# Gate logits taken from extra columns of two products that run anyway, in the second stage of an attention and mixture-of-experts kernel

## The reference

```python
def _mha(x, Wqkv, bqkv, Wo, bo): ...        # 4 heads of 32 
    return o @ Wo.T + bo
def _moe(x, Wg, W1, b1, W2, b2):
    logits = xf @ Wg.T
    idx = jnp.argmax(logits, axis=-1)
    for e in range(E):                       # 8 experts, one per token
        h = jax.nn.relu(xf @ W1[e] + b1[e])
        out = out + m * (h @ W2[e] + b2[e])
y = _layer_norm(x + _mha(x, ...), g1, be1)
z = _layer_norm(y + _moe(y, ...), g2, be2)
```

## Time and profile before

| | us |
|---|---|
| median of 3 runs (lowest, highest) | 1230.01 (1229.64, 1231.98) |
| the profiled execution, its own time | 1225.95 |
| its span in the profile | 1224.1 |
| stage one, until the first transfer of stage two | 803.3 |
| stage two, from there to the last scatter's end | 233.5 |
| of it, slots 6 to 13, mean of one | 12.17 |

### The profile page before, as it was taken

The page is one execution under the profiler, slowest core; times in us unless marked ns, Lnnn a source line. Parts: engine busy times, 40 slices in busy tenths (PEclk is TensorE's granted clock), DMA queues, the critical chain, the costliest instruction groups (busy, mean ns, idle before and its releaser), DMA issues. The chain is left out here.

```text
span 1224.1 us, 49591 instructions
## 1 busy us (share of the span) xinstructions
PE 1099.8 (90%) x17489; PEld 898.3 (73%) x17489; DVE 958.7 (78%) x4172; ACT 922.7 (75%) x3404; POOL 874.6 (71%) x703
## 2 busy tenths in 40 slices
PE   4799999999999999999999999947999972799991
PEld 2688888888888888888888887725877772688881
DVE  6898898998898898898988987546888854376763
ACT  2789989989989889899899897836877641466660
POOL 2777877877877877877777875554677776178885
PEclk9999999999999999999999999969989975799996
DMA  6776766766766666767667666353242124574100
GB/s 197 207 179 158 183 165 167 185 167 161 182 165 172 171 173 166 179 158 181 166 163 183 156 159 180 92 183 93 63 135 92 71 85 161 161 202 138 58 32 25
DMA packets 111027, 180.88 MB, mean 148 GB/s; under 512 B 19726, under 2 KB 64177, under 8 KB 110656
## 3 DMA queue, kind: packets, MB, share of 16 engines
q1 hardware_dynamic: 102944, 158.53, 50.1%
q0 software_dynamic: 6400, 16.82, 3.8%
q10 hardware_dynamic: 1440, 2.36, 0.8%
HBM read 35.20 MB, written 24.73 MB: 49 GB/s over the span
## 5 line engine op out<-in xcount | busy, mean ns | idle before, releaser
L612 POOL TENSOR_TENSOR qk<-mm,sw 128x1024 f32<-128x1024 f32 x128 | 305.1, 2384 | 103.2 <-DMA sw<-mm 102.6
L685 ACT ACTIVATE pr<-sm,mn 128x96 f32<-128x96 f32 x1024 | 368.7, 370 | 0.3 <-DVE mn L513 0.3
L618 POOL TENSOR_TENSOR pr<-pr,ri 128x768 f32<-128x768 f32 x128 | 189.2, 1478 | 66.7 <-DVE ri L540 66.6
L501 DVE TENSOR_TENSOR mm<-bank,cos 128x512 f32<-128x512 f32 x256 | 175.3, 685 | 70.1 <-PE bank L324 58.3
L685 ACT ACTIVATION_READ_ACCUMULATOR pr<-sm,mn 128x1 f32 x1024 | 201.6, 197 | 0.0
L513 DVE CUSTOM_DVE_ANT_0 sm<-bank,msk 128x96 f32<-128x96 f32 x1024 | 190.9, 251 | 3.4 <-PE bank L350 3.4
L502 DVE TENSOR_TENSOR mm<-bank,sin 128x512 f32<-128x512 f32 x256 | 173.8, 679 | 0.0
L377 PE MATMUL bank<-pT,vw 96*64 96x64 f32 x4096 | 148.2, 226 | 0.0
L377 PEld LDWEIGHTS bank<-pT,vw 96*64 96x64 f32 x4096 | 130.6, 138 | 17.2 <-issue 6.0
L676 ACT ACTIVATE pT<-bank 96x512 f32<-96x512 f32 x256 | 137.3, 588 | 0.2 <-PE bank L392 0.2
L392 PE MATMUL bank<-ident,pr 128*96 128x128 f32 x1024 | 133.1, 273 | 0.0
(11 more groups left out here) (206 smaller groups left out, 2485.6 us busy)
## 6 DMA issues: line engine op xcount, KB each, us to landing
sw<-mm SPq DMA_DIRECT2D x512, 128.0 KB, 2.4
vw<-vn SPq DMA_DIRECT2D x128, 192.0 KB, 2.6
vw<-vn SPq DMA_DIRECT2D x128, 128.0 KB, 2.3
rr<-sorted_scratch SPq DMA_DIRECT2D x72, 192.5 KB, 2.6
vw<-vn SPq DMA_DIRECT2D x96, 64.0 KB, 2.2
xt<-in_x SPq DMA_DIRECT2D x16, 256.0 KB, 4.2
x_scratch<-x SPq DMA_DIRECT2D x16, 256.0 KB, 2.6
rr<-x_scratch SPq DMA_DIRECT2D x16, 256.0 KB, 3.2
```

Source lines behind the costliest of these rows:

```text
L501: dve.tensor_tensor(mm[s % 2][:, 0, j, :], PJ[u % 2][:, :], cos[:, :], ALU.mult)
L612: pool.tensor_tensor(qk[i % 2][:, :, 32:], mm[i % 2][:, 0, :, :], sw[i % 2][:, :, :], ALU.add)\
L618: pool.tensor_tensor(t, t, ri[i % 2][:, :].unsqueeze(2).to_broadcast([P, 8, WK]), ALU.mult)\
L685: ins = act.activation(pr[i % 2][:, h, p, :], ms_[i % 2][:, h, p, :], ACT.Exp, scale=-1.0, bias=mn[i % 2][:, h, p:p + 1], accum_out=sums[i ...
```

## The change

Since u is a linear function of the input and of the attention output, the columns of Wg can be carried along. With G = g1 * Wg less its column mean (the norm's mean taken out), the logits are r * (u @ G) + be1 @ Wg. The change

- widens the value product from 128 to 136 columns per group (`wve`: the value weights and G) and the output product likewise (`woe`: the output weights and their product with G); their sum is made by the same addition that makes `uu`, now 4 x 136 wide. Value and output products take two banks each (`wide`), so the ring is laid out anew (`r_pos`, `r_prev`);
- drops the transposes t3, their copy yT, the gate product and the copy of its result; the gate now multiplies eight columns of `uu` by r and adds be1 @ Wg, two DVE operations, and waits for POOL's norm of the same slot;
- moves the gate of a quad from slot s+5 to s+4, rank and scatter from s+6 to s+5: the loops end one slot earlier (20 instead of 21);
- moves the rank counts behind the value product on PE, the be1 x W1 columns into the bank of the output product, `w1l` of an expert to the slot after its high part, and the load of the expert's weights a slot later;
- adds one small ACT copy (eight columns of the value product into `h2`), and lets the input's transposed copy hT be plain, with the biases corrected once (`fbn`) at the stage's start; `prepare()` moves ahead of the first statistics on DVE and a new `gate()` takes its place.

The core of the diff, in the order ring, POOL, PE, ACT, DVE:

```diff
-    FIRST, LAST = -3, NQ + 6
+    FIRST, LAST = -3, NQ + 5
+        for kind, u in (("t1", s), ("q", s), ("k", s), ("pt", s - 2), ("v", s), ("rk", s - 5), ("wo", s - 3)):
+                size = 2 if kind in ("v", "wo") else 1
+                pos += pos % size if kind != "rk" else 1 - pos % 2
...
+                        pool.wait_ge(s_le, 2 * (s - 6) + 1)
...
-                u = s - 6
+                u = s - 5
...
-                u = s - 5
-                    pe.wait_ge(s_cy, u + 1)
-                    dst = bank("t3", u)
-                    for j in range(4):
-                        ins = pe.transpose(dst[:, j * P:(j + 1) * P], quad_rows(u)[:, j, 0:C], ident[:, :])
...
-                    for j in range(4):
-                        ins = pe.matmul(dst[:, j * NE:(j + 1) * NE], yT[:, j * P:(j + 1) * P], wg, start=True, stop=True)
+                    for g in range(4):
+                        ins = pe.matmul(dst[:, g // 2, g % 2, :], hT[u % 2][:, g * P:(g + 1) * P], wve[:, :],
+                                        start=True, stop=True)
...
+                        ins = pe.matmul(dst[:, j // 2, j % 2, :], oT[u % 2][:, j * P:(j + 1) * P], woe[:, :],
                                         start=True, stop=True)
...
-                    act.activation(yT[:, :], ring("t3", u)[:, :], ACT.Identity, scale=gcol[:, 0:1], bias=gcol[:, 1:2])\
-                        .then_inc(s_ye, 1)
+                    act.activation(halves(h2[u % 7][:, :, C:]), blocks("v", u)[:, :, :, C:], ACT.Copy).then_inc(s_ve, 1)
...
+                    dve.tensor_tensor(halves(uu[u % 2][:, :, :]), blocks("wo", u), halves(h2[u % 7][:, :, :]), ALU.add)\
+                        .then_inc(s_u, 1)
...
-                u = s - 5
-                    dve.wait_ge(s_r, r_use[("lg", u)] + 1)
+                u = s - 4
+                    dve.wait_ge(s_ln, norms(s))
...
-                    dve.tensor_copy(lg[:, :, :], ring("lg", u)[:, 0:4 * NE].rearrange("p (j e) -> p j e", j=4))\
+                    dve.tensor_tensor(lg[:, :, :], uu[u % 2][:, :, C:], rs[s % 2][:, 1, :].unsqueeze(2).to_broadcast([P, 4, NE]),
+                                      ALU.mult).then_inc(s_le, 1)
+                    dve.wait_ge(s_le, 2 * u + 1)
+                    dve.tensor_tensor(lg[:, :, :], lg[:, :, :], lgb[:, :].unsqueeze(1).to_broadcast([P, 4, NE]), ALU.add)\
```

More of the change, by code:

```diff
@@ L742, in phase2 @@
     hc = [sbt(p2, f"hc{n}", [P, 4, C]) for n in range(2)]
-    h2 = [sbt(p2, f"h2{n}", [P, 4, C]) for n in range(7)]
+    h2 = [sbt(p2, f"h2{n}", [P, 4, CE]) for n in range(7)]
     hT = [sbt(p2, f"hT{n}", [P, 4 * P]) for n in range(2)]
@@ L754, in phase2 @@
     oT = [sbt(p2, f"foT{n}", [P, 4 * P]) for n in range(2)]
-    uu = [sbt(p2, f"uu{n}", [P, 4, C]) for n in range(2)]
-    yT = sbt(p2, "yT", [P, 4 * P])
+    uu = [sbt(p2, f"uu{n}", [P, 4, CE]) for n in range(2)]
+    wve = sbt(p2, "wve", [P, CE])
+    woe = sbt(p2, "woe", [P, CE])
+    woT = sbt(p2, "woT", [P, C])
+    wgs = sbt(p2, "wgs", [P, NE])
+    lgb = sbt(p2, "lgb", [P, NE])
+    fbn = sbt(p2, "fbn", [P, 3])
     lg = sbt(p2, "lg", [P, 4, NE])
@@ L1018, in bank @@
             def bank(*w):
-                n = r_use[w]
-                if n >= 4:
-                    kind, v = order[n - 4]
+                for kind, v in sorted(r_prev[w]):
                     pe.wait_ge(emptied[kind], v + 1)
-                return RING[n % 4]
+                return ring(*w)
             pe.wait_ge(s_l2, 16 * 6)
@@ L1085, in _ @@
                 if quad(u):
-                    pe.wait_ge(s_cy, u + 1)
-                    dst = bank("t3", u)
-                    for j in range(4):
-                        ins = pe.transpose(dst[:, j * P:(j + 1) * P], quad_rows(u)[:, j, 0:C], ident[:, :])
+                    pe.wait_ge(s_oh, u + 1)
+                    dst = bank("rk", u)
+                    for j in range(5):
+                        o = dst[:, j * NE:(j + 1) * NE]
+                        for i in range(min(j, 3) + 1):
+                            ins = pe.matmul(o, trb[:, 0:P] if i == j else trb[:, P:2 * P], oh[u % 2][:, i, :],
+                                            start=(i == 0), stop=(i == min(j, 3)))
                     ins.then_inc(s_r, 1)
@@ L1120, in _ @@
                     pe.wait_ge(s_oe, 4 * u + 4)
-                    dst = bank("wo", u)
+                    bank("wo", u)
+                    dst = blocks("wo", u)
+                    e = u - 2
+                    if 0 <= e < NE:
+                        pe.wait_ge(s_ws[e % 2], 16 * (e // 2 + 1))
+                        for c in range(4):
+                            pe.matmul(pair("wo", u)[:, 0, 2 * CE + c:2 * CE + c + 1], w1s[e % 2][:, c * P:(c + 1) * P],
+                                      gcol[:, 1:2], start=True, stop=True)
                     for j in range(4):
-                        ins = pe.matmul(dst[:, j * C:(j + 1) * C], oT[u % 2][:, j * P:(j + 1) * P], wfo,
+                        ins = pe.matmul(dst[:, j // 2, j % 2, :], oT[u % 2][:, j * P:(j + 1) * P], woe[:, :],
                                         start=True, stop=True)
@@ L1216, in _ @@
                     act.wait_ge(s_r, r_use[("k", u)] + 1)
-                    act.activation(kT[u % 2][:, :], ring("k", u)[:, :], ACT.Identity, bias=fb[:, 1:2]).then_inc(s_ke, 1)
+                    act.activation(kT[u % 2][:, :], ring("k", u)[:, :], ACT.Identity, bias=fbn[:, 1:2]).then_inc(s_ke, 1)
                 u = s - 2
```

135 lines of the change are left out of this document (71 added, 64 removed).

## The result

The changed kernel took 1236.87 us (median of 20 runs, 1230.74 to 1241.65), the kernel before 1230.99 in runs beside them (20 runs, 1225.23 to 1235.98): a ratio of 1.0049 [1.0034, 1.0064]. The forecast was 1214.6 and faster.

What follows compares the result with a forecast made beforehand. PE was taken to bound slots 6 to 13, DVE close behind, and POOL the end. Gains of 7.2 + 1.1 + 2.0 + 5.1 = 15.4 us gave 1214.6 us, in a range of 1207 to 1224.

Steps and rivals of the forecast that it cites:

- DVE becomes the bound: Slots 6 to 13: PE's cut leaves DVE binding, 12.17 to 11.27 us a slot, 7.2 us gained over eight.
- rival 1: PE stays the bound through its pauses; steady gain 0 to 1 us, whole kernel 1223 us; chance 0.15.
- The clock: Sign of being wrong: PE's granted clock in slots 6 to 13 falls below about 0.85.
- DVE's list: DVE's own work in slots 6 to 13: 10.83 plus 0.24 makes 11.07 us a slot, before 0.2 for rank counts.
- Rival 3: Where POOL is late, its operations hold DVE's gate, about 1 us a slot over ten slots: 1225 us; chance 0.04.
- The other sign: Sign of being wrong: DVE's first gate operation shows idle time behind POOL's norm.
- Rival 2: PE at 1.2 GHz in the whole stage: 19 us lost, 5.1 gained, 1244 us; chance 0.05.
- rival 5: A new bank wait in the ring eats the slots' gain, the norm's wait the end's: 1229 us; chance 0.03.
- The start: Start of stage two: `prepare()` runs in DVE's first wait, POOL's norm covers `gate()`; between -1 and +1, taken as 0.
- The end: From norm(15) to the last scatter's end: POOL's list has one quad of scatters less, 5.1 us gained, between 4 and 8.
- Slots 14 and 15: No expert's weights there, POOL's list binds: 10.6 us a slot, 1.1 us gained, between 0 and 2.
- this term was +2.0: POOL comes out of the steady part less late: 2.0 us gained, between 0 and 3.

Runs made afterwards that it cites:

- 76 records ahead: Changed kernel plus 38 small 32x32 products, results unread, on PE ahead of the slot loop: 1225.49 us, ratio 0.9964 to the kernel before.
- three buffers: Changed kernel with three instead of two buffers for the experts' weights: 1236.22 us, ratio 1.0056 to the kernel before.
- ACT's order: Changed kernel with ACT's copies of keys and transposed probabilities ahead of the exponent: 1233.14 us, ratio 1.001 to the kernel before.
- 300 records ahead: 150 small 32x32 products on PE ahead of the slot loop: changed kernel 1235.95 us (ratio 1.0057), kernel before 1229.43 us (0.9983).
- the last three sets: Runs of both kernels with half the small products, each twice as wide, and of combined edits; the unchanged kernel before took 1278 to 1294 us beside them.
- the first two: Sets with the first four experiments and the scan of records ahead; beside them the kernel before took 1230.56 and 1231.22 us.

## Why the prediction was wrong

*The step that failed* is "DVE becomes the bound", and in it rival 1's answer, "DVE's 2 us of room hide most of a pause". A slot does not end with the longest list of one engine, but with the later of that list and the loop DVE, ACT, PE, DVE. The loop is some 9.7 us long when nothing disturbs it, 1.5 below the list (the estimate above). A pause costs it not 2 us but 4.2, since the products behind it run at the lower clock. Both numbers stood in the earlier trace rows (1.74 of pause, 2.00 for the product); they were never put into the chain that ends at DVE's addition. DVE's waits on PE, 10.7 us in the earlier trace rows, were taken for PE's load, which the cut removes; but the pauses of over 0.8 us in those slots alone sum to 6.3 us (1.68, 0.83, 2.09, 1.74), and their slow rows come on top; these the cut does not remove. This term was +7.2 and measured -7.5. DVE's waits for PE were to be under 0.5 us a slot and were 1.95.

*The clock* was named as the sign of being wrong (below about 0.85) and came to 0.84. The runs add that it falls behind the pause: after three of the four pauses in P by V the next two steps are the slow ones (1.87 and 2.16 us), after the first only the second (1.82). Over 935.80 to 940.00 the granted clock is 0.50. With more work on PE it was 0.87 in slots 6 to 13, and they took as long (104.3 us). The Trainium skill (TensorE: Matmul & The Clock Gate, "A second HAM failure mode: psum-queue depth-cycling") tells of frequent short idle spells that swing the clock; the trace agrees with that much, while in these slots the idle spells in front of the slow rows have no bank or other releaser named.

*Rival 1* was the right mechanism with a chance of 0.15 and too small a price: it let the steady part give back the cut, no more, and came to 1223. That less work makes the records of a slot fewer, and thereby moves where pauses fall, was not in it at all. The place alone is 11 us. Which kernel drew the better place was luck either way; the 15.4 us of gain came at none of four.

*DVE's list*: 11.07 forecast without the counts, 11.16 measured. The counts' own wait, taken as 0.2 a slot, is 0.8 us in eight, 0.1 a slot. The sum is right in part by luck: `h` (L1381) rose from 949 to 1185 ns and the ranks' product (L1399) from 455 to 758, while the copy of the rows fell from 601 to 324. None of the three operations was changed. Some of its groups, 871.57 to 976.46, answer to the earlier trace rows:

```profile
L1381 DVE TENSOR_TENSOR h<-h,modp 128x512 f32<-128x512 f32 x8 | 9.5, 1185 | 0.3
...
L1399 DVE TENSOR_TENSOR rk<-rk,oh 128x32 f32<-128x32 f32 x8 | 6.1, 758 | 0.0
...
L1350 DVE TENSOR_TENSOR uu<-bank,h 128x544 f32<-128x544 f32 x8 | 5.7, 717 | 0.0
```

*Rival 3, the gate held by POOL,* did not happen in steady slots. The two added operations over all 16 quads, minimum, median and maximum in ns:

```profile
L1418 DVE TENSOR_TENSOR lg<-uu,frs x16: 157/164/1152, 859.4 to 1037.4; 128x32 f32<-128x32 f32 x16
L1421 DVE TENSOR_TENSOR lg<-lg,lgb x16: 191/192/971, 859.6 to 1037.6; 128x32 f32<-128x32 f32 x16
```

The maxima are of one quad, at 985.93 and 987.11, where POOL's rows L989 and L994 ran from 985.85 to 988.04. The Trainium skill (SBUF — State Buffer, "Who interferes with whom") has DVE and GpSimd contend for a shared port pair; there the trace agrees, an operation of 0.16 us takes 1.15. Over 16 quads the two means are 0.23 and 0.24 us, above the 0.2 that was named as a sign of being wrong, by this one quad. The other sign came too, but only in the last three quads: DVE waits 3.9 to 4.0 us each for POOL's norm in front of the gate, 11.8 in all. Before, it waited there for PE's gate product, 3.86 and 5.39 us in the last two.

*Rival 2* (the lower clock throughout) and *rival 5* (a new wait for a bank in the ring) did not come: slot 5 and the stretch from slot 14 to norm(15) run at a clock of 1.00, and the one wait for a bank, that of the counts for the probabilities' copy (5.4 us in eight slots), delays nothing by itself: P by V behind it needs the same copy.

*The start* was taken as 0 within 1 and cost 4.4: slots 2 to 4 took 9.7, 13.7 and 10.7 us, with pauses of 1.59 and 1.98 at 836.23 and 841.73. With 76 records ahead the same slots took 7.5, 9.4 and 11.3. This is the place again, in a part of the stage for which the prediction had no pauses.

*The end*: the scatter quad was saved as forecast (5.1); the 3.5 us given back are POOL's waits for DVE, which had PE's low clock (0.63) in front of them. POOL was counted as the bound there; it was one only from norm(17) on. *Slots 14 and 15* were to gain 3.1 us and took 1.1 more: pauses of 0.84 and 1.91 us at 988.30 and 992.44 fell there, and POOL came out of the steady part later, not earlier. Its norm(15) stands 6.2 us behind slot 15's start (986.98 to 993.18), before 5.3; this term was +2.0 and came out as -0.9.

## What to carry to other kernels

When a cut makes one engine less busy, follow the loop through the engines, with every pause and its slow rows in it, and not only the longest list: an idle reserve in a list is no reserve in the loop. Where small instructions run densely, an edit that changes their number moves the pauses of the stream, and moves the time by several us either way; before calling such an edit faster or slower, shift the stream by a few dozen empty products and measure each version at three or four places; keep the shift short, since 150 of them brought a pause of their own here. The place was worth 11 us, more than the edit, and the best version was the change at another place (0.9964 [0.9944, 0.9985]).

## What the runs showed of the hardware

- TensorE stops for up to 3.3 us inside a run of small products with no releaser in the trace, at places that recur with its instruction stream: in the changed kernel and in two runs with the same stream (three buffers, ACT's order) 44, 32, 20 and 8 records are left in every second slot. From one of these pauses to the next it issues 632 matmul records (and as many weight loads); the distances in the kernel before, 505, 631 and 631, and the 125 records between the pauses at 875.17 and 882.75 are near one, four and five times 126. Not every such place shows a pause.
- The pause needs neither data nor a bank: in the two runs with 300 records ahead it came among products that only read the identity and wait for no semaphore, 3.96 and 3.97 us. What it waits for is not shown; that it is the delivery of instructions fits with the regular distance and with the trickles, and is an inference.
- Behind such a pause the next steps run at the lower clock level: 0.50 over 935.80 to 940.00, where the output product takes 2.16 us instead of 1.17.
- In the last three sets the score products came in groups of 2 to 11 records every 0.71 to 0.79 us beside POOL's indirect scatters, and the kernel before took 47 to 63 us longer. Half the instructions for the same columns gave 1.6 to 2.4% back. The scatters themselves took their usual 0.97 us meanwhile. Why these sets differ from the first two is open.
